# Cross-attention and mixture-of-experts block: order of the loads (rs last, bv and the experts' weights behind x of batch 1) and of the work on every engine

## The reference

```python
def reference(...):
    # attention, 16 heads of 32
    hs = layernorm(x)
    q = hs @ Wq.T + bq;  k = clean(ctx) @ Wk.T + bk;  v = clean(ctx) @ Wv.T + bv
    scores = clip(q k^T / sqrt(32), -50, 50), masked keys at -50
    probs = softmax(scores);  att = probs @ v
    delta = clip(rs, 0, 0.3) * (att @ Wo.T + bo)
    x = x + layernorm(delta) * gamma + beta
    # 8 experts of 16 hidden units, the best two kept
    y = layernorm(x)
    gate = softmax(y @ router.T), all but the two largest set to 0
    out = x + sum_e gate_e * (silu(y @ down_e.T) @ up_e.T)
```

## Time and profile before

| | us |
|---|---|
| median of three runs | 186.54 (184.55 to 188.71) |
| the profiled execution | 186.6 |
| its span, first to last instruction | 183.9 |
| TensorE busy | 171.8 |
| VectorE busy | 137.5 |
| ScalarE busy | 113.4 |
| GpSimd busy | 101.8 |

### The profile page before, as it was taken

The page is one execution under the profiler, slowest core; times in us unless marked ns, Lnnn a source line. Parts: engine busy times, 40 slices in busy tenths (PEclk is TensorE's granted clock), DMA queues, the critical chain, the costliest instruction groups (busy, mean ns, idle before and its releaser), DMA issues.

```text
span 183.9 us, 3557 instructions
## 1 busy us (share of the span) xinstructions
PE 171.8 (93%) x1212; PEld 126.2 (69%) x1212; DVE 137.5 (75%) x306; ACT 113.4 (62%) x231; POOL 101.8 (55%) x157
## 2 busy tenths in 40 slices
PE   7999779979998899999999999989999999999990
PEld 7486558846654378884888486666778598889860
DVE  3788498997999558998238584467898898773993
ACT  3038706984853875489986592769734787778410
POOL 5032089995837528999966984416133595364100
PEclk9999999999999999999999999999999999999999
DMA  6999995000157596455991526430409458000248
GB/s 168 354 384 300 399 250 207 4 0 4 62 150 279 136 284 172 124 179 204 302 215 67 173 59 197 148 95 18 114 18 329 127 221 235 4 2 0 86 176 309
DMA packets 18049, 30.13 MB, mean 164 GB/s; under 512 B 3056, under 2 KB 8176, under 8 KB 17776
## 3 DMA queue, kind: packets, MB, share of 16 engines
q1 hardware_dynamic: 18032, 29.92, 51.5%
HBM read 19.95 MB, written 9.96 MB: 163 GB/s over the span
## 4 chain that ended last, share of the span: by engine, by line
PE 44%; DVE 23%; DMA 13%; SPq 8%; issue 4%; POOL 3%; ACT 3%; DVEq 0%; ACTq 0%
PE ps L469 38%; DMA xs<-x 6%; DMA rz_scratch<-rz 3%; DVE xs L1223 3%; PE ps L574 3%; DVE stage L1147 3%; DVE ln_st L1231 3%; DVE hst_lo L1088 2%; DMA x_scratch<-x_turned 2%; PE ps L560 2%; DVE v_sb L1132 2%; POOL attt_lo L1509 2%; DMA wk<-rz_scratch 1%; SPq L360 1%; DVE wk L1157 1%
## 5 line engine op out<-in xcount | busy, mean ns | idle before, releaser
L1509 POOL TENSOR_TENSOR attt_lo<-wk,attt_hi 128x512 fp32r<-128x512 f32 x16 | 21.7, 1373 | 13.6 <-ACT attt_hi L801 13.5
L469 PE MATMUL ps<-hst_hi,wq_hi 128*128 128x512 f32 x64 | 26.2, 409 | 2.3 <-DVE hst_lo L1088 2.3
L469 PE MATMUL ps<-wo_hi,attt_hi 128*128 128x512 f32 x64 | 25.9, 405 | 0.2 <-POOL attt_lo L1509 0.2
L1505 POOL TENSOR_TENSOR xs<-xs,beta_bc 128x512 f32<-128x512 f32 x16 | 20.7, 1320 | 9.4 <-DMA beta_bc<-beta 8.1
L469 PE MATMUL ps<-hst_hi,wq_lo 128*128 128x512 f32 x64 | 25.3, 395 | 0.0
L469 PE MATMUL ps<-wo_hi,attt_lo 128*128 128x512 f32 x64 | 25.3, 395 | 0.0
L469 PE MATMUL ps<-wo_lo,attt_hi 128*128 128x512 f32 x64 | 25.3, 395 | 0.0
L469 PE MATMUL ps<-hst_lo,wq_hi 128*128 128x512 f32 x64 | 25.2, 394 | 0.0
L764 ACT ACTIVATE hs<-xs,ln_bias,ln_rstd 128x512 f32<-128x512 f32 x16 | 12.1, 807 | 11.5 <-POOL ln_bias L1497 11.5
L783 ACT ACTIVATE stage<-ps 128x1024 f32<-128x1024 f32 x16 | 15.9, 1025 | 5.3 <-PE ps L546 5.3
L1147 DVE TENSOR_SCALAR stage<-stage,exp_max 128x1024 f32<-128x1024 f32 x16 | 15.3, 959 | 5.1 <-ACT stage L783 5.1
(11 more groups left out here) (111 smaller groups left out, 387.6 us busy)
## 6 DMA issues: line engine op xcount, KB each, us to landing
wk<-rz_scratch SPq DMA_DIRECT2D x32, 128.0 KB, 2.8
out<-xs SPq DMA_DIRECT2D x16, 256.0 KB, 2.2
xs<-x SPq DMA_DIRECT2D x3, 1024.0 KB, 8.9
x_scratch<-x_turned SPq DMA_DIRECT2D x6, 512.0 KB, 2.6
x_turned<-x_scratch SPq DMA_DIRECT2D x24, 128.0 KB, 2.9
hs_scratch<-hs_turned SPq DMA_DIRECT2D x2, 1024.0 KB, 5.1
hs<-hs_scratch SPq DMA_DIRECT2D x8, 256.0 KB, 5.4
wk<-wk_t SPq DMA_DIRECT2D x4, 256.0 KB, 5.9
```

What stands on the lines that cost most here:

```text
L469: last = pe.matmul(dst, w, m, start=start and i == 0, stop=stop and i == n - 1, skip_group_check=unseen)
L1505: pool.tensor_tensor(xt, xt, beta_bc[:, :], ALU.add).then_inc(xb_ok, 1)
L1509: pool.tensor_tensor(attt_lo[:, :, c, :], att[:, c, :].rearrange("p (t n) -> p t n", t=NT), attt_hi[:, :, c, :].bitcast(F32), ALU.subtract ...
```

## The change

small_load loses the DMA of rs, which becomes rs_load, the last load of the first group. bv_load and experts_load come directly behind x1_load, then wo_load and load(2), and behind that gamma_load, bo_load and rs_load. The lists of calls of all five engines and the bank lists are new; every call of before is there again, once. Steps for an up product on ScalarE are added (experts_seed, finish on ScalarE, the tuple UP_ON_SCALAR), but the tuple is empty, so none of them is called. The core of the diff:

```diff
             def small_load():
...
+            def rs_load():
                 sp.dma_start(rs_raw[:, :], rs.broadcast_to([P, 1])).then_inc(rs_in, 16)
...
             small_load()
             x1_load()
+            bv_load()
+            experts_load()
+            wo_load()
+            load(2)
             gamma_load()
-            wo_load()
             bo_load()
-            experts_load()
-            bv_load()
-            load(2)
+            rs_load()
             spread_out(0, 0)
             spread_in(0, 0)
             spread_out(0, 1)
             spread_in(0, 1)
             hs_send(2)
+            load(3)
             hs_fetch(2)
-            load(3)
+            x1_send(0, 0)
             spread_out(1, 0)
+            x1_fetch(0, 0)
+            spread_in(1, 0)
+            hs_send(3)
+            x1_send(0, 1)
+            hs_fetch(3)
+            x1_fetch(0, 1)
             spread_out(1, 1)
...
```

VectorE's list up to product(0, 0):

```diff
             clean_limited(1)
-            clean_finite(1)
             tile_stats(0, 0)
             tile_stats(0, 1)
+            clean_finite(1)
+            tile_stats(0, 2)
+            tile_stats(0, 3)
             clean_marks(2)
-            tile_stats(0, 2)
             clean_limited(2)
+            hs_lo(0, 0)
             clean_finite(2)
             clean_marks(3)
-            tile_stats(0, 3)
-            hs_lo(0, 0)
+            clean_limited(3)
             hs_lo(0, 1)
-            clean_limited(3)
+            clean_finite(3)
             wq_low(0)
-            clean_finite(3)
             wq_low(1)
+            hs_lo(0, 2)
+            hs_lo(0, 3)
             wq_low(2)
             wq_low(3)
+            tile_stats(1, 0)
             mask_limits()
-            residual_scale()
-            tile_stats(1, 0)
-            hs_lo(0, 2)
-            hs_lo(0, 3)
             tile_stats(1, 1)
             tile_stats(1, 2)
             tile_stats(1, 3)
-            centre_wo(0)
-            centre_wo(1)
-            centre_wo(2)
             value_blocks(0)
             value_blocks(1)
             tile_stats(2, 0)
             tile_stats(2, 1)
             tile_stats(2, 2)
+            residual_scale()
+            centre_wo(0)
+            centre_wo(1)
+            centre_wo(2)
+            clip(0, 0)
+            clip(0, 1)
...
```

## The result

The kernel after takes 189.46 us (median of 5, 187.55 to 194.89), the kernel before 186.87 in the same measurement (184.55 to 188.71): ratio 1.021, 95% interval 1.015 to 1.027. So it is slower, by 1.5 to 2.7%. The forecast was 186.4, no change (0.2 us less), with a range of 182.3 to 190.2: the time lies in the range, but the kernel got slower beyond the noise where next to no change was forecast.

The account below looks back on a forecast made before the run. TensorE, busy 93% of the span, was taken as the bound, with only its gaps and the end able to move. Terms -1.3 + 1.7 - 1.05 + 0.6 - 0.15 + 0 = -0.2 gave 186.4 us, range 182.3 to 190.2.

Parts of the forecast that it names:

- part 3: Up to the first projection: gaps of 0.78 and 0.67 go, GpSimd's chain and the sums cost 0.2 each; -1.05 us.
- part 5: The middle: small gaps may go (-1.1), down(0, 2) comes 0.65 late, down(1, 2) waits 0.3; -0.15 us.
- Base and what can move: TensorE's products stay the same; the change can only remove gaps (at most 6.1 us), add some, or alter the end.
- Part 1: First 24 us: TensorE's gaps of 2.27 and 0.24 go, new waits cost 1.2; -1.3 us (-2.0 to -0.5).
- Part 2: The loads: waits around x of batch 2 and centring wo add 2.8, a 1.07 gap goes; +1.7 us.
- Part 4: Before query(2, 0): load(3) now between hs_send(2) and hs_fetch(2), so x of batch 3 is late; +0.6 us.
- Part 6: The end, from down(3, 3) to the last finish: 9.9 us against 10.0 before; 0, with 0.5 either way.
- (a): Rival: the gaps go and none come, x of batch 2 lands at 28.8 to 29; 182.5 us, chance 0.25.
- (b): Rival: GpSimd bounds batch 0, at att_lo(0, 3) before project(0, 0) and before query(2, 0); 190.9 us, chance 0.13.
- (c): Rival: loads not directly behind x, so x of batch 2 lands no sooner than 32.8; 187.9 us, chance 0.12.

Follow-up runs that it names:

- The single swap: The kernel before with hs_lo(0, 2) and hs_lo(0, 3) ahead of tile_stats(1, 0) on VectorE: 186.49 us, ratio 1.004.
- the long execution: The kernel after, unchanged: the profiled execution of its first measurement, the longest of five, span 193.2 us.

## Why the prediction was wrong

The steps that failed are part 3, put at -1.05 and measured at +0.4 in gaps; part 5, put at -0.15 and measured at +1.6; and the granted clock, which stood in the sum at nothing, for no reason given, and took 1.7 us. In part 3 the input that was not followed comes from VectorE by way of att_hi and att_lo; in part 5 two round trips through memory, of x1 and of the reciprocals, were priced too low. The figures are those of the profiled execution of 190.56 us.

**Base and what can move.** Right that only gaps count; incomplete, since it took TensorE's rate as given. The granted clock was not a term of the sum and took 1.7 us of the profiled execution.

**Part 1, -1.3.** Right in its own rows: 0.42 + 0.28 stand where the earlier trace rows had 2.51, -1.8. What it took for granted is that TensorE's time there is worth its length. The single swap gave 1.004. VectorE starts on x of batch 1 and is not free before 38.5, in the earlier trace rows already: after the 2.40 us no idle time over 0.26 stands ahead of its work. hs_transpose(1, 3) starts at 39.85, against 39.32 before.

**Part 2, +1.7.** x of batch 2 was awaited until 29.58, forecast 30.7; beta until 30.97, forecast 31.9; centring took 4.3, forecast 5.1 (the short value throughout came out). New gaps 0.82 + 1.27 against a forecast of 2.8, so +1.0 after the 1.07 that went. The size was missed by 0.7, on the good side, and that is in part luck: in the long execution of the same kernel the two gaps are 1.84 + 4.03, beyond the part's upper bound. By "GPSIMD Engine Reference", section 8 (Key points), of the Trainium skill every pair of that kind would be long. Here the subtractions were short (0.49 to 0.52) beside GpSimd, and long (1.36 to 1.53) in the longer execution of the same kernel, so the trace agrees at times. The clips were long beside GpSimd in three profiles of four (two of them took 2.42, 3.26 and 3.42 us, and 1.40 with GpSimd idle), a term that I hadn't priced.

**Part 3, -1.05.** This step failed. The gaps of 0.78 and 0.67 went, but 1.84 came, and 1.7 behind it for the clock: +0.4 and +2.1 where -1.05 was forecast. GpSimd's chain was forecast to end at 59.2 and ended at 60.01, but not by its own work: it stood 1.61 us for att_hi, which the forecast had at nothing. I had not followed the input of att_lo back: att_hi, product(0, 2), and ahead of that VectorE's two operations at 1.5 us each. Before, they took 0.46 and 0.58:

```profile
54.31 0.46 DVE L1248 TENSOR_SCALAR gamma_bc<-gamma_bc,rs_sb 128x512 f32<-128x512 f32 x1
57.32 0.58 DVE L1296 TENSOR_SCALAR bo_bc<-bo_bc,w_mv 128x512 f32<-128x512 f32 x1
```

That the 0.78 before sums(1, 0) went was luck of this execution: in ten of the fourteen profiles with this order 0.5 to 2.2 us stand there, for x of batch 3, which the prediction followed to query(2, 0) and not to clip(1, 1).

**Part 4, +0.6.** Measured 0.40. Right.

**Part 5, -0.15.** Wrong by 1.8. The gaps that went are 1.0 (0.67 and twice 0.16 of them in the part's own rows); those that came are 1.07, 0.25, 1.07 and 0.25, 2.64, so +1.6, past the upper bound of 1.5. x1_fetch behind hs_fetch(3) was named as the place, at up to 1.3, and took 1.07, where I took half; down(1, 2) was put at 0.3 and took 1.07, since I took the delay of product(3, 0) from its place in the queue and not from the reciprocals' round trip that starts 8 us earlier (132.86 against 140.80).

**Part 6, 0.** 9.9 forecast, 9.9 measured (175.3 to 185.2).

**The sum.** In gaps: -1.8 + 1.0 + 0.4 + 0.4 + 1.6 = +1.6, as counted above; forecast -0.2. In the clock +1.7, behind the last finish +0.7, in what isn't found +0.8, around the span -0.9: +3.9 or so, beside the 4.0 measured. **The rivals:** (a) had it right that the old gaps go, and not that none come. (b) named att_lo(0, 3) before project(0, 0), at 190.9. The place and nearly the time are right, the mechanism is not: att_lo(0, 3) was the last input, but GpSimd was late by VectorE's products and not by the price of its own operations. (c) did not happen: x of batch 2 was in at 29.6.

## What to carry to other kernels

A gap of the busiest engine is worth its length only if the engine that ends the next wait has slack; look for the stretch in which a second engine has no idle time, here VectorE from 22 to 38 us. For each operation that is moved, follow every input of what waits for it back to its start, the round trips through memory above all, and price operations of VectorE that come to lie beside GpSimd at their long value. When a sum of gaps doesn't explain the time, read the granted clock next to the gaps: here an idle time of 1.84 us cost 1.7 us more by the clock behind it.

## What the runs showed of the hardware

- Granted clock: in the twenty profiles TensorE has eight idle times of 2.59 us and more (2.59, 3.89, 3.96 twice, 4.03 twice, 5.68, 8.03), and it was 0.50 from within or just behind each of them, for some 3 to 7 us. Of the fifteen from 1.83 to 2.35 us it was so with six (1.84, 1.92 twice, 2.00, 2.02, 2.35); behind the others, as the 2.27 us at 24 in the kernel before, 2.35 in one kernel at 102 and 2.21 in another at 71, it stayed at 1.00. A pair of 0.99 and 1.27 us was followed by 0.50 in one profile while a pair of 1.73 and 1.25 was not in another. "TensorE: Matmul & The Clock Gate", section "Part 1: The HAM clock gate", of the Trainium skill says that the clock knows a full and a half rate alone; the table agrees, 0.50 and 1.00 with mixtures only where a stretch holds the change.
- A clip of 128x1024 f32 in place took 0.70 us with GpSimd idle, 1.2 to 1.7 beside its additions; a one-input operation of 128x512 f32 0.49, and beside GpSimd 1.4 to 1.5 in some executions and 0.49 to 0.52 in others.
- x of batch 3 (1 MB) took 5.5 to 11.4 us from issue to landing in the fourteen profiles of the kernel after and its variants that keep clip(1, 1) in its place.
- Around the span lie 2.5 us in the kernel before and its variants (median of 87 executions, of which 25 are at 1.7 to 1.9) and 1.7 in the kernel after and its variants (median of 81, all at 1.7 to 2.1). It goes with the engines' orders and not with the order of the loads; why, I don't know.
